# Attention and expert layer on one core: choice of expert before the second half of h, halved stores, a smaller first load, and a repeated product between two stages

## The reference

```
x = x + layernorm(attention(layernorm(x)))         # 16 heads of 8, causal linear attention
x = x + layernorm(ffn(layernorm(x)))

def ffn(x):                                        # x: 4096 x 128
    logits = x @ w_router.T                        # 16 experts
    top_idx = argmax(logits)                       # top 1
    scores = sigmoid(logits) * one_hot(top_idx)
    gate, up = split(einsum(scores * x, gate_up_proj))   # 2 x 256 per expert
    expert_out = (up * silu(gate)) @ down_proj
    shared = (silu(x @ w_gate.T) * (x @ w_up.T)) @ w_down.T
    return shared + expert_out.sum(over experts)
```

## Time and profile before

| | |
|---|---|
| median of three runs | 345.31 us (344.48, 345.31, 346.79) |
| profiled execution | 347.56 us, its span 345.8 us |
| mean granted TensorE clock | 0.913 |
| busy share of the span | TensorE 77%, VectorE 83%, ScalarE 54%, GpSimd 56% |
| attention, routing, experts | to about 155, to 235.6, to the end |
| scatters L474 | 32, 0.99 us each |
| TensorE busy from 230 to 240 | 0.05 us |

### The profile page before, as it was taken

The page is one execution under the profiler, slowest core; times in us unless marked ns, Lnnn a source line. Parts: engine busy times, 40 slices in busy tenths (PEclk is TensorE's granted clock), DMA queues, the critical chain, the costliest instruction groups (busy, mean ns, idle before and its releaser), DMA issues.

```text
span 345.8 us, 6250 instructions
## 1 busy us (share of the span) xinstructions
PE 264.6 (77%) x1465; PEld 184.2 (53%) x1465; DVE 286.4 (83%) x1138; ACT 186.6 (54%) x572; POOL 192.7 (56%) x221
## 2 busy tenths in 40 slices
PE   3459999999998995638887988821999999999000
PEld 1125556555554553325555655521999889988000
DVE  5998999999999999996998787640379999999930
ACT  2524656565665552257666664203899888885000
POOL 5056777767775863200054556570007888888870
PEclk9988999999999998967999899985899999999655
DMA  6999900000000000000011111126950101110000
GB/s 187 374 426 396 396 4 0 2 3 0 2 0 2 2 0 0 1 1 2 1 62 64 63 62 64 64 100 229 355 166 18 35 31 43 41 36 29 25 2 0
DMA packets 13668, 28.39 MB, mean 82 GB/s; under 512 B 1950, under 2 KB 10150, under 8 KB 12610
## 3 DMA queue, kind: packets, MB, share of 16 engines
q1 hardware_dynamic: 10448, 21.57, 17.1%
q0 software_dynamic: 3040, 6.37, 5.4%
q10 hardware_dynamic: 146, 0.07, 0.1%
HBM read 15.38 MB, written 13.60 MB: 84 GB/s over the span
## 4 chain that ended last, share of the span: by engine, by line
PE 39%; DVE 24%; POOL 18%; issue 12%; DMA 4%; ACT 1%; POOLq 0%; ACTq 0%; SPq 0%; another core or an unknown queue 0%; DVEq 0%
PE banks L1009 13%; POOL out L490 10%; POOL rows L484 6%; PE banks L1028 5%; PE banks L1100 5%; DVE hT L814 2%; PE banks L1037 2%; PE banks L1134 2%; POOL sorted_rows L474 2%; DVE stats L641 2%; DMA rows<-in_x 2%; PE banks L997 2%; DVE num L740 1%; DVE rows L857 1%; DVE stats L849 1%
## 5 line engine op out<-in xcount | busy, mean ns | idle before, releaser
L1009 PE MATMUL banks<-kv,upto 128*128 128x512 f32 x128 | 63.5, 621 | 1.3 <-POOL kv L449 1.3
L449 POOL TENSOR_TENSOR kv<-qk,vv 128x1024 f32<-128x1024 f32 x32 | 62.4, 1950 | 2.5
L1134 PE MATMUL banks<-xsT,w_now 128*128 128x128 f32 x376 | 52.6, 284 | 0.4 <-DVE hT_e L948 0.4
L490 POOL DMA_INDIRECT out<-rows,token_i x47 | 46.8, 997 | 9.8 <-issue 8.2
L443 POOL TENSOR_TENSOR qk<-ex,rl 128x256 f32<-128x256 f32 x32 | 23.3, 727 | 47.0 <-ACT ex L546 47.0
L1134 PEld LDWEIGHTS banks<-xsT,w_now 128*128 128x128 f32 x376 | 47.1, 197 | 1.2 <-issue 0.7
L474 POOL DMA_INDIRECT sorted_rows<-rows,slot_i x32 | 31.7, 992 | 28.7 <-DVE slot_i L804 20.7
L718 DVE TENSOR_TENSOR prod<-banks,qk 128x1024 f32<-128x1024 f32 x32 | 38.9, 1216 | 2.1 <-PE banks L1009 1.5
L740 DVE TENSOR_REDUCE num<-prod 128x128 f32<-128x1024 f32 x32 | 38.7, 1208 | 0.3 <-DVE den L735 0.3
L948 DVE TENSOR_TENSOR hT_e<-silu_e,banks 128x256 f32<-128x256 f32 x47 | 19.4, 412 | 19.8 <-ACT silu_e L623 16.1
L484 POOL TENSOR_TENSOR rows<-rows,yn 128x128 f32<-128x128 f32 x40 | 19.1, 477 | 28.0 <-DVE yn L940 26.1
(11 more groups left out here) (158 smaller groups left out, 640.0 us busy)
## 6 DMA issues: line engine op xcount, KB each, us to landing
sorted_rows<-rows SPq DMA_DIRECT2D x3, 1950.0 KB, 13.3
rows<-sorted_rows SPq DMA_DIRECT2D x11, 520.0 KB, 6.3
w_exp<-in_gate_up SPq DMA_DIRECT2D x4, 1024.0 KB, 19.7
w_exp_down<-in_down SPq DMA_DIRECT2D x4, 512.0 KB, 19.7
rows<-in_x SPq DMA_DIRECT2D x1, 1024.0 KB, 11.1
rows<-in_x SPq DMA_DIRECT2D x1, 768.0 KB, 8.4
out<-rows,token_i POOLq DMA_INDIRECT x47
sorted_rows<-rows,slot_i POOLq DMA_INDIRECT x32
```

Source lines behind the costliest of these rows:

```text
L449: nc.gpsimd.tensor_tensor(kv[:, u, :].rearrange("p (h m d) -> p h m d", h=NH, m=HD), k, v, ALU.mult).then_inc(s_kv, 1)
L490: nc.gpsimd.indirect_dma_start(out=out_rows, out_offset=bass.IndirectOffsetOnAxis(ap=token_i[:, j - 1:j], axis=0), in_=rows[:, j - 1, 0:D] ...
L1009: ins = nc.tensor.matmul(ps_s[u % 2][:, cols], upto[:], kv[:, u, cols], start=True, stop=True)
L1134: ins = nc.tensor.matmul(ps_gue[u % 2][:, c * P:(c + 1) * P], w_now[:, u % 2, c * P:(c + 1) * P], xsT[:, u % 2, :], start=True, stop=True)
```

## The change

1. In groups 6 and 7 (`NG - 2` and `NG - 1`) VectorE now makes `h(0)`, then the whole choice, then `h(1)`; TensorE counts the ranks ahead of the down product in both. Before, group 6 had the choice around and behind `h(1)` with the ranks behind the down product, and group 7 had the choice ahead of both halves.
2. The last group's down product goes to two banks, two tiles in each; ScalarE stores each half by itself, and GpSimd waits per scatter for the half that it needs.
3. SP loads the sorted table in 13 pieces, of 1, 3, and then 4 tiles; ScalarE waits for the second piece ahead of tile 1.
4. Behind the turn of the tile ranks TensorE multiplies `ident` by 512 columns of the shared weights eight times into a bank that nobody reads: twice at once, once after each of the last four scatters, on a semaphore that GpSimd now raises after each, and twice after all scatters have landed.

```diff
+        w_g_u = w_all[:, 0:2 * F]
...
+        ps_last = [ps_y2, ps_t2]
-        ps_turn = bank[5]
+        ps_turn, ps_idle = bank[5], bank[4]
...
@@ SP @@
-            quads = [(q, min(q + 4, ST)) for q in range(0, ST, 4)]
-            for n, (j0, j1) in enumerate(quads):
+            pieces = [(0, 1), (1, 4)] + [(q, min(q + 4, ST)) for q in range(4, ST, 4)]
+            for n, (j0, j1) in enumerate(pieces):
...
@@ GpSimd @@
                 for t in range(GT * g, GT * (g + 1)):
+                    if g == NG - 1:
+                        pool.wait_ge(s_sh_out, g + 1 + (t - GT * g) // 2)
                     nc.gpsimd.indirect_dma_start(
...
+                    if g == NG - 1:
+                        pool.sem_inc(s_last_scatters, 1)
...
@@ ScalarE, step2 @@
                     act.wait_ge(s_sh, s + 1)
-                    nc.scalar.copy(rows[:, tiles(GT * s, GT), D:2 * D],
-                                   ps_y2[:].rearrange("p (t d) -> p t d", d=D)).then_inc(s_sh_out, 1)
+                    if s < NG - 1:
+                        nc.scalar.copy(rows[:, tiles(GT * s, GT), D:2 * D],
+                                       ps_y2[:].rearrange("p (t d) -> p t d", d=D)).then_inc(s_sh_out, 1)
+                    else:
+                        for half in range(2):
+                            act.wait_ge(s_sh, s + 1 + half)
+                            nc.scalar.copy(rows[:, tiles(GT * s + 2 * half, 2), D:2 * D],
+                                           ps_last[half][:, 0:2 * D].rearrange("p (t d) -> p t d", d=D)
+                                           ).then_inc(s_sh_out, 1)
...
@@ ScalarE, step3 @@
-                        act.wait_ge(s_loaded, q + 2)
+                        act.wait_ge(s_loaded, q + 3 if q >= 0 else 1)
+                    elif j == -3:
+                        act.wait_ge(s_loaded, 2)
...
@@ VectorE, h_and_choice_steps @@
-                final = isinstance(s, int) and s == NG - 1
-                if not final:
-                    yield h(0)
+                routed_first = s >= NG - 2
+                yield h(0)
                 dve.wait_ge(s_logit, s + 1)
                 yield nc.vector.tensor_reduce(top[:, u, :], logits, AX, ALU.max).then_inc(s_top, 1)
-                if not final:
+                if not routed_first:
                     yield h(1)
...
-                if final:
-                    yield h(0)
+                if routed_first:
                     yield h(1)
...
@@ TensorE, step2 @@
-                if isinstance(s, int) and s == NG - 1:
+                if s >= NG - 2:
                     rank()
                 if live(s, NG):
                     pe.wait_ge(s_h, 2 * s + 2)
                     at_least(pe, s_sh_out, s)
                     for k in range(GT):
                         for f in range(FC):
-                            ins = nc.tensor.matmul(ps_y2[:, k * D:(k + 1) * D], hT[:, f, k * P:(k + 1) * P],
-                                                   w_d[:, f, :], start=f == 0, stop=f == FC - 1)
-                    ins.then_inc(s_sh, 1)
-                if live(s, NG) and not (isinstance(s, int) and s == NG - 1):
+                            if s < NG - 1:
+                                into = ps_y2[:, k * D:(k + 1) * D]
+                            else:
+                                into = ps_last[k // 2][:, (k % 2) * D:(k % 2 + 1) * D]
+                            ins = nc.tensor.matmul(into, hT[:, f, k * P:(k + 1) * P], w_d[:, f, :],
+                                                   start=f == 0, stop=f == FC - 1)
+                        if k == GT - 1 or (s == NG - 1 and k == 1):
+                            ins.then_inc(s_sh, 1)
+                if live(s, NG) and s < NG - 2:
                     rank()
...
@@ TensorE, behind the turn of the tile ranks @@
+            for n in range(GT + 2):
+                if 0 < n <= GT:
+                    pe.wait_ge(s_last_scatters, n)
+                elif n > GT:
+                    pe.wait_ge(s_scattered, 16 * NT)
+                for _ in range(1 if 0 < n <= GT else 2):
+                    nc.tensor.matmul(ps_idle[:], ident[:], w_g_u[:, 0:4 * P], start=True, stop=True)
```

More of the change, by code:

```diff
@@ L349, in build @@
         s_scattered = sem("rows_scattered")
+        s_last_scatters = sem("last_scatters_begun")
         s_tile_rank = sem("tile_ranks_ready")
@@ L419, in _ @@
                 sp.dma_start(rows[:, j0:j1, :], sorted_tiles[:, j0:j1, :]).then_inc(s_quad[n % 4], 16)
-            for n in range(len(quads), len(quads) + 4):
+            for n in range(len(pieces), len(pieces) + 4):
                 sp.wait_ge(s_quad[n % 4], 16 * (n // 4))
@@ L596, in _ @@
             step1(NT + 1, 1)
-            run_steps(act, step2, -1, 1, 5, NG, 2, 2)
+            for g in range(-1, NG):
+                step2(g, g % 2)
             act.wait_ge(s_experts, 1)
@@ L901, in _ @@
             step1(NT, 0)
-            run_steps(dve, step2, -1, 1, 5, NG + 1, 2, 2)
+            for g in range(-1, NG + 1):
+                step2(g, g % 2)
             dve.wait_ge(s_slot, NG)
@@ L1113, in _ @@
             pe.wait_ge(s_y_out, NT)
-            run_steps(pe, step2, 0, 1, 7, NG, 2, 2)
+            for g in range(NG):
+                step2(g, g % 2)
             pe.wait_ge(s_tile_rank, 1)
             nc.tensor.matmul(ps_turn[0:1, 0:P], tile_rank[:], ident[:], start=True, stop=True).then_inc(s_tile_row, 1)
+            for n in range(GT + 2):
[5 more added lines that the diff above has]
+                    nc.tensor.matmul(ps_idle[:], ident[:], w_g_u[:, 0:4 * P], start=True, stop=True)
             def step3(q, u, parity):
```

## The result

The changed kernel takes 344.54 us (median of 20 runs, 342.99 to 345.89) where the kernel before, timed beside it in 20 runs, takes 346.92 (344.27 to 348.08). The ratio is 0.9938 with a 95% interval of 0.9916 to 0.9960: faster by 0.6%, 1.4 to 2.9 us. The three runs of the kernel before that stood ahead of the prediction, median 345.31, were at the low side of its spread. The profiled execution of the changed kernel took 344.77 us with a span of 342.8, 3.0 less than the span before.

A forecast was written before the change was run, and what follows sets the result against it. The bound was the chain of waits from last scatter through first load to ScalarE's `xs` of tiles 0 and 1, plus TensorE's half clock. 0.4 + 0.8 + 1.4 = 2.6 us off gave 342.7 against 345.31, own range 341.9 to 343.4.

The forecast's parts named there:

- The terms: Gains forecast: 0.4 us from first load issued earlier, 0.8 from one-tile first load, 1.4 from the repeated product.
- counts: GpSimd's semaphore raises behind the scatters: three on the path at 0.06 us each, 0.2 lost; bounds 0 and 0.5 each.
- the clock falls all the same: TensorE into the expert stage: clock not held despite the repeated product, 1.2 us gained in all, 344.1.
- the 0.20: Joint chance that first tile is not ahead (343.5), clock is not held (344.1) or GpSimd's counts cost more (344.0).
- The first rival: Expert stage's half-clock stretch longer in timed runs, each us costing 0.5: total 3.6 to 4.1 us, 341.2 to 341.7; chance 0.30.
- The slower rival: Repeated product at half clock blocks TensorE's queue ahead of the first transposes: 347.6, or 348.9 with further waiting; chance 0.05.

The follow-up runs named there:

- the second trace: The changed kernel run once more with no edit, for another trace; ratio 0.9924 to the kernel before.
- e10: The changed kernel with the last group's shared rows in one bank and one copy, no wait ahead of each scatter; ratio 0.9965 to the kernel before.
- e8: The changed kernel with group 7 in its old order, the choice ahead of both halves of hT; ratio 0.9939 to the kernel before.
- e4: The kernel before with only the sorted-table loads changed to pieces of 1, 3, then 4 tiles; ratio 0.9956 to the kernel before.
- e7: The changed kernel with pieces of 2, 2, then 4 tiles and two more products behind the first load; ratio 0.9940 to the kernel before.
- e1: The changed kernel without the repeated product and without GpSimd's counts; ratio 0.9949 to the kernel before.
- e6: The changed kernel with two more repeated products on TensorE behind a wait for the first load; ratio 0.9905 to the kernel before.
- e2: The kernel before with only the repeated product and GpSimd's counts added; ratio 0.9988 to the kernel before.

## Why the prediction was right or wrong

**The size of the whole** was near: 2.6 us or 0.75% forecast, 0.62% measured (0.40 to 0.84). That is in part luck. The terms were 0.4, 0.8 and 1.4; in the first trace they came as 1.2, 0.2 and 0.2 (together 1.6), in the second as 1.0, 0.9 and 1.3 (3.2), and the timed gain (2.4 us between the medians) lies between such executions.

**The absolute time** was not near: 342.7 against 344.54, above the 343.4 that closed my own range. The step that failed there is "It lay 2.25 above the median, so against 345.31 the forecast is 342.7": the base was the median of three runs of a kernel whose runs spread over 3.8 us, and 20 runs put it at 346.92. From there 2.6 us lead to 344.3. I had the warning in hand, with a profiled execution 2.25 above that median. And "About 1%, 3.45 us, is what can be told from no change" was too coarse: a change of 0.6% came clear of the noise.

**Part 1** (0.6 before counts; measured 0.9 to 1.2 up to the first load in ten traces with the new order, 0.3 in e10). The step that failed is "`hT` half 1 of group 6 now runs at 215.8 to 216.4 where it ended at 216.1". It starts 1.90 us behind group 5's slots as before, since `top` starts 0.68 behind them and not 1.11 (an idle time of 0.34 that the trace before puts down to nothing on the core is gone, and no run says why), and the choice ends as `silu_g` half 1 ends. So down did not move, and with the ranks no longer behind it group 7's `silu_g` half 1 starts 0.28 sooner (9.06 against 9.34) and not 0.25 later. The step behind it held: `taken` of group 7 stands behind `hT` half 1, which waits for `silu_g` half 1 in the first trace and in e8. So the 0.5 us between 0.28 sooner and 0.25 later is what `taken` had more than forecast: 0.94 against 0.4 (0.64 in the second trace). In the kernel before, VectorE was itself the late one: it got to `top` only at 222.38, as the slots of group 6 ended at 222.47, while `silu_g` half 0 (from 220.84) and the logits (from 221.0) were ready. Group 6's own scatters begin 2.6 us sooner in two traces, near the forecast 2 to 2.5, and only 1.3 to 1.4 in the other nine, which have ScalarE's late store of the last section; GpSimd waits ahead of group 7 either way.

**Part 2** (0, less 0.2 for counts; measured 0 and 0 in the first trace, 0.67 gained in e10's comparison). The step "two half copies and a wait per scatter are over before 228.5" took the copy's start behind the down product from one trace; it varies by 1.3 us. The counts are free, three times 0.06 too much.

**Part 3** (0.8): right in size, 0.8 in e4 alone and 0.75 to 0.9 in seven of the eight other traces with this split; in the first trace of the changed kernel 0.2.

**Part 4** (1.4): the mechanism was right, the certainty wrong. The failed step is "They leave TensorE no pause like the one in which the clock fell. The first transpose is wanted at 238.2, so TensorE waits for it and not the other way round". I counted the wait as harmless. Between the last product and tile 1 TensorE has one transpose in 2.5 to 3.2 us, and in or right behind that pause the clock falls in some executions. Where it holds, `xs` 1 to 6 takes 7.19 to 7.35 us (8.05 in e7, where the products block), 1.1 to 1.9 less than without the product (8.43 to 9.12); where it falls, 0.2 to 0.6 remain against the kernel before. I had this as a bound ("the clock falls all the same") with too little of the 0.20 on it. The first rival, a longer slow stretch without the product, is real as well: e1 shows it, with 9.12 (half clock to about 245.9, 5.8 us from its first dense matmuls, against 3.3 before); it costs 0.6 us at tile 6, less than the 0.5 per us that the rival has. How often the kernel before has it is not shown. The Trainium skill, TensorE: Matmul & The Clock Gate, Part 1, says that one kernel meets different numbers of slow matmuls from run to run. The two traces of the changed kernel agree: 8.31 us with a fallen clock and 7.19 with a held one, for the same tiles.

**The slower rival** did not come: the products ran at full clock in every trace but e8, where the clock had fallen at the end of the pause ahead of them and came back while they ran, and in the changed kernel they held up no transpose. What it named, products that block the start, is what e7 shows, at full clock and for 1.1 us.

What stays open: why the second load landed 0.6 us late in one trace of nine, why the clock held in three and fell in three of the pauses of 2.1 to 3.4 us, and how much of the 0.6% each part is worth by time alone; no ratio of a single part but e4's is clear of 1, and the changed kernel with and without the product (0.9938 and 0.9949) are not told apart.

## What to carry to other kernels

A product that keeps the clock up across a wait has to reach to the next dense work, not to the event before it: list every wait between the two, here the landing of the second load, and let the last of the repeats be released by the event before it, here the landing of the first load (e6). When a step is said to be covered, ask again once the change itself has moved that cover. And take the base of a forecast of 1% from more than three runs, or measure from a point just ahead of the change in the trace.

## What the runs showed of the hardware

ScalarE's store of group 6 starts 2.09 us behind the start of the down product in all three traces with the old order (before, e2, e4). With the new order it does so in one of eleven, once at 2.64, and nine times at 4.4 to 4.5, with an idle time that the trace puts down to nothing on the core:

```profile
217.13 2.05 PE L1120 MATMUL banks<-w_ffn,hT 128*128 128x128 f32 x16 [0.29 <-DVE hT L831]
...
221.58 0.59 ACT L595 COPY rows<-banks 128x512 f32<-128x512 f32 x1 [4.65 <-remote]
```

Group 7's `silu_g` half 0, behind it on ScalarE, starts 7.59 us behind group 5's `slot_i` there and 6.45 in the changed kernel's first trace, yet the slots of group 7 come at 13.5 to 13.8 either way. The product's modelled end says nothing of it. I have no cause for it; no kernel was run on it.
